# Routing of an audio tower's second expert mixture, worked off group by group within the attention before it

## The chip, the cores and the metric
One core of one Trainium2 chip. The metric is the device time of one execution in microseconds, the median of several runs. TensorE multiplies matrices (its granted clock is either 1.2 or 2.4 GHz; the profile gives it as a share of 2.4), VectorE and ScalarE work elementwise and reduce, GpSimd (POOL in the profile) works elementwise, more slowly, and issues indirect transfers, and the queue of SyncE (SP) issues the other transfers. Each engine has one queue and works it off in order; they wait for each other by semaphores.

## The reference, cut to what matters
64 sequences of 95 positions (96 in the kernel, one of padding) with 128 channels pass four layers. The kernel's first two phases do a token mixer, a retention layer and a first mixture; the change hardly touches them. Then come
```
h = h + attention(layernorm(h))   # over the 64 sequences at each position, 8 heads of 64
xf = layernorm(h).reshape(-1, 128)
z = swiglu5(xf @ shared_w1 + shared_b1) @ shared_w2 + shared_b2
w, idx = top_k(softmax(xf @ gate_w + gate_b), 2);  w = w / sum(w)
y = sum over the two chosen of 16 experts of w * (swiglu5(xf @ expert_w1 + b1) @ expert_w2 + b2)
h = h + y + z
```
Attention itself works across the batch: for one position the 64 sequences are queries and keys of each other. A position's result is final as soon as its step is done, so nothing in the mixture's norm and choice of experts has to wait for the other positions.

## The kernel before, in words
`hT` holds h in SBUF, channels on partitions, 64 x 96 tokens. `build` calls four phases one after the other; each is a block with a queue for every engine, and all engines meet at its end. At the start of a phase GpSimd clears the semaphores of the phase before.

**Attention** (`phase_attention`, L1432 to L1938) takes 4 positions, 256 tokens, a step: 24 steps. Body g of each engine's queue works at four steps at once: the scores and probabilities of step g, the projections of g + 1, the norm of g + 2 (`ln1`), and the output, the norm behind it (`ln2`) and the store of h of g - 1 and g - 2. `steps` writes out bodies 0 and 1, a hardware loop of ten pairs, and bodies 22 to 25. The order within a body is written by hand. What the prediction follows: TensorE's projections (L1549), scores (L1565 to L1576), turning and applying the probabilities (L1588, L1600), output product (L1611), and the turn of the normalised rows (`to_columns`, L660), which stands in the middle of the next scores; ScalarE's squares of the keys (L1683), normalisation (L1703) and its copy of h into `hg` (L1697); VectorE's keys (L1833, L1834), distances (L1841), shift (L1848 to L1852), probabilities (L1858 to L1864), store (L1884), scaled mean (L1890); GpSimd has only the inverse roots of two norms (L646).

**The second mixture** (`phase_second_mixture`, L1941 to L2630) first takes 12 groups of 512 tokens (8 positions of all 64 sequences) through this chain: ScalarE copies the group out of hT (`copy_in`, L2269), TensorE turns it into rows (L2155), VectorE takes mean and variance (`statistics`, L2420), GpSimd the inverse root (L2382), ScalarE normalises and repeats the rows (L2276, L2280), TensorE turns them into columns (L2164), ScalarE copies (`copy_x`, L2295), TensorE multiplies by the gate (`route`, L2173), VectorE finds the best two (`best`, L2439 to L2450, `chosen`, L2456 to L2468), TensorE counts the tokens before each one by a product with a triangle of ones (`prefix`, L2200), VectorE gets the positions of its 1024 rows in `slots` (`places`, L2478 to L2494), ScalarE the two shares by a sigmoid (L2287), and GpSimd sends the rows there with 8 indirect transfers (`send`, L2393). Each group's ranks build on the counts of the one before (`carry`). Beside this the shared expert is worked off: `shared_up` (L2182), `shared_clip` (L2500, L2502), `shared_silu` (L2301), `shared_act` (L2510), `shared_down` (L2192, and L2193, which adds h), `keep` (L2306). VectorE also prepares the experts' parameters, scales the weights (L2564), and SP writes them to DRAM (L2097). Behind the last group VectorE computes from the counts which expert each block of 128 rows belongs to (L2568 to L2591); TensorE turns this table, VectorE copies it out (L2595), and SP reads it.

Then come 111 blocks: SP loads rows and an expert's weights, TensorE turns the rows (`turn`, L2209), goes up (`ups`, L2217) and down (`down`, L2225), VectorE clips (L2607, L2608) and multiplies (L2616), ScalarE copies, does the SiLU (L2319) and scales (L2357), GpSimd sends the result back (L2400). The end adds the two rows of each token to the shared expert's result and stores it (L2627, L2629, L2081). The waits on `s_sent` hold the first load of rows until every row has been sent:
```
for sent in s_sent:
    sp.wait_ge(sent, 16 * 2 * GB * (NG // RX))
```

## Time and profile before
| | us |
|---|---|
| median of three runs | 2220.99 (2220.93 to 2224.79) |
| the profiled execution | 2223.54 |
| its span in the trace | 2221.7 |
| attention, from 1349.2 | 456.4 |
| second mixture up to its first block, from 1805.6 | 187.9 |
| 111 blocks, from 1993.5 | 192.1 |
| sums and stores at the end, from 2185.6 | 36.1 |

Over the span TensorE is busy for 87%, VectorE for 69%, ScalarE for 59%, GpSimd for 40%. The rest, up to 1349 us, is the two phases before. A row of a group of instructions gives line, engine, operation, what is written and read, shapes and count, then busy time and the mean of one, then the engine's idle time right before them and what ended it. A row in order of time begins with the start and the length in us; the bracket at its end is the idle time before it and its releaser. "PE" is TensorE's multiplication, "ACT" ScalarE, "DVE" VectorE. A wait that ends with "issue" or "remote" has no engine behind it that the profile shows.

### The profile page before, as it was taken

What the parts mean: (1) busy time and instruction counts of PE and PEld (TensorE: products, weight loads), DVE (VectorE), ACT (ScalarE), POOL (GpSimd) and SP (SyncE); (2) the same over time, 40 slices, a digit from 0 to 9 for tenths busy, and PEclk for the clock granted to TensorE, in tenths of its full rate; (3) what the DMA queues carried; (4) which work ended last, traced back from release to release, by engine and by line L of the source; (5) the groups of instructions that cost most, each with busy time, mean ns of one, the idle gap of its engine ahead of it and who ended that gap; (6) DMA issues with size and microseconds to landing.
All of it is one profiled execution on the core that took longest, in us unless ns stands there. A gap on an engine that the chain in (4) does not pass through costs nothing. (4 is left out here: it accounts for less than half of the span.)

```text
span 2221.7 us, 47490 instructions
## 1 busy us (share of the span) xinstructions
PE 1939.6 (87%) x16570; PEld 1359.7 (61%) x16570; DVE 1534.3 (69%) x3495; ACT 1312.7 (59%) x2355; POOL 891.5 (40%) x744
## 2 busy tenths in 40 slices
PE   5899999979998999999999997999999956657772
PEld 4678887845554566666666664666666634546661
DVE  4534455348886999999999984777777746645554
ACT  2445456445553677677767775777777746535551
POOL 0000000015553888888888882000000017655552
PEclk9999999989998999999999999999999967678876
DMA  8860010069920000000000000000000022126664
GB/s 281 321 234 29 21 30 11 1 239 411 413 94 11 10 11 10 10 10 10 10 10 10 10 10 22 2 0 0 0 0 0 1 50 90 43 67 183 183 181 176
DMA packets 87338, 177.84 MB, mean 80 GB/s; under 512 B 25917, under 2 KB 63214, under 8 KB 77846
## 3 DMA queue, kind: packets, MB, share of 16 engines
q1 hardware_dynamic: 78646, 160.11, 21.2%
q0 software_dynamic: 6624, 12.70, 1.7%
q10 hardware_dynamic: 1920, 3.11, 0.4%
q8 instruction: 86, 1.41, 0.3%
q14 instruction: 62, 0.51, 0.1%
HBM read 82.00 MB, written 94.86 MB: 80 GB/s over the span
## 5 line engine op out<-in xcount | busy, mean ns | idle before, releaser
L1146 ACT ACTIVATE b_pool_b<-b_pool_a,c_b 128x1024 f32<-128x1024 f32 x384 | 436.8, 1150 | 176.6 <-DVE b_pool_a L1379 153.9
L1216 POOL TENSOR_TENSOR b_pool_c<-b_pool_b 128x512 f32<-128x512 f32 x384 | 492.3, 1290 | 110.3 <-ACT b_pool_b L1146 64.8
L1379 DVE TENSOR_TENSOR b_pool_a<-b_p_s,c_shares 128x1024 f32<-128x1024 f32 x384 | 454.6, 1216 | 49.9 <-PE b_p_s L985 47.5
L983 PE MATMUL b_p_s<-c_x_hi,c_w_hi 128*128 128x512 f32 x384 | 296.4, 772 | 1.8 <-DVE b_pool_a L1379 1.8
L646 POOL TENSOR_TENSOR d_ln_rstd<-d_ln_var,d_ln_power 128x2 f32<-128x2 f32 x48 | 34.1, 711 | 418.9 <-DVE d_ln_var L642 414.0
L990 PE MATMUL b_p_y<-b_pool_c,c_w 128*128 128x512 f32 x384 | 196.7, 593 | 0.0
L990 PE MATMUL b_p_p<-b_pool_c,c_w 128*128 128x512 f32 x384 | 194.8, 591 | 0.0
L984 PE MATMUL b_p_s<-c_x_lo,c_w_hi 128*128 128x512 f32 x384 | 153.4, 399 | 0.0
L1268 DVE TENSOR_TENSOR b_pool_b<-b_p_s,b_decay 96x384 f32<-96x384 f32 x256 | 124.6, 546 | 41.5 <-PE b_p_s L854 41.3
L248 POOL COPY a_work<-a_vec 128x64 f32<-128x64 f32 x4 | 1.2, 306 | 378.5 <-PE a_p_A L339 222.9
L985 PE MATMUL b_p_s<-c_x_hi,c_w_lo 128*128 128x512 f32 x384 | 152.0, 396 | 0.0
L2400 POOL DMA_INDIRECT e_again<-e_by,e_xb x111 | 108.4, 977 | 92.0 <-ACT e_by L2357 50.9
L983 PEld LDWEIGHTS b_p_s<-c_x_hi,c_w_hi 128*128 128x128 f32 x384 | 73.3, 191 | 86.1 <-issue 77.2
L984 PEld LDWEIGHTS b_p_s<-c_x_lo,c_w_hi 128*128 128x128 f32 x384 | 73.6, 192 | 83.2 <-issue 83.0
L2393 POOL DMA_INDIRECT slots<-e_rows_x,e_pos x96 | 95.9, 999 | 39.9 <-issue 27.3
L1833 DVE TENSOR_SCALAR d_kk<-d_p_p,d_mu 128x256 f32<-128x256 f32 x96 | 46.0, 479 | 87.5 <-PE d_p_p L1549 87.5
L2319 ACT ACTIVATE e_bswish<-e_bgate,e_wb 96x128 f32<-96x128 f32 x111 | 54.8, 493 | 74.3 <-issue 49.2
L323 PE MATMUL a_p_A<-a_R,a_V 128*128 128x128 f32 x496 | 96.1, 275 | 0.0
L325 PE MATMUL a_p_A<-a_R,a_V 128*128 128x128 f32 x496 | 95.9, 275 | 0.0
L1176 POOL TENSOR_TENSOR b_yrs<-b_yve,b_power 96x32 f32<-96x32 f32 x15 | 81.4, 5427 | 35.0 <-DVE b_yve L1277 35.0
L527 DVE COPY a_work<-a_p_A 128x512 f32<-128x512 f32 (+1 forms) x32 | 21.6, 676 | 99.6 <-PE a_p_A L325 99.6
L985 PEld LDWEIGHTS b_p_s<-c_x_hi,c_w_lo 128*128 128x128 f32 x384 | 72.7, 189 | 18.8
(324 smaller groups left out, 4706.8 us busy)
## 6 DMA issues: line engine op xcount, KB each, us to landing
slots<-b_pool_c SPq DMA_DIRECT2D x55, 1040.0 KB
e_wb<-e_weights SPq DMA_DIRECT2D x111, 164.0 KB
band_scratch<-a_work SPq DMA_DIRECT2D x16, 1024.0 KB, 5.3
a_work<-band_scratch SPq DMA_DIRECT2D x16, 1023.5 KB, 7.6
a_raw<-in_Wc SPq DMA_DIRECT2D x16, 512.0 KB, 3.6
e_xb<-slots SPq DMA_DIRECT2D x111, 65.0 KB
c_shares<-c_share_lists SPq DMA_DIRECT2D x12, 512.0 KB, 3.8
e_yb<-e_again SPq DMA_DIRECT2D x12, 512.0 KB, 5.9
```

The source lines that it names most:

```text
L323: nc.tensor.matmul(bank[:, cols], V[:, j, :], R[:, f, 0:2 * NB], start=True, stop=False, skip_group_check=True)
L325: last = nc.tensor.matmul(bank[:, cols], V[:, j + 1, :], R[:, f, NB:3 * NB], start=False, stop=True, skip_group_check=True)
L983: nc.tensor.matmul(p_h[q % SLOTS][:, 0:WIDE], w1_hi[:, q, :], x_hi[s][:, :], start=True, stop=False)
L984: nc.tensor.matmul(p_h[q % SLOTS][:, 0:WIDE], w1_hi[:, q, :], x_lo[s][:, :], start=False, stop=False)
L985: nc.tensor.matmul(p_h[q % SLOTS][:, 0:WIDE], w1_lo[:, q, :], x_hi[s][:, :], start=False, stop=True)\
L990: nc.tensor.matmul(p_o[s][:, 0:WIDE], fw2[:, q, :], both[q % SLOTS][:, :], start=(q == 0), stop=(q == FQ - 1)).then_inc(s_down, 1)
L1146: nc.scalar.activation(hid[q % SLOTS][:, :, :], gelu_in[q % SLOTS][:, :, :], ACT.Gelu, bias=b1[:, q:q + 1]).then_inc(s_ge, 1)
L1216: nc.gpsimd.tensor_tensor(both[q % SLOTS][:, :], hid[q % SLOTS][:, 0, :], hid[q % SLOTS][:, 1, :], ALU.add).then_inc(s_bo, 1)
L1268: v.tensor_tensor(sm[n % 2][:, j, :], p_s[j][0:SP, 0:4 * SP], decay[:, j, :, :].rearrange("t a s -> t (a s)"), ALU.mult).then_inc(s_sm, 1)
L1379: v.tensor_tensor(gelu_in[q % SLOTS][:, :, :], p_h[q % SLOTS][:, 0:WIDE].unsqueeze(1).to_broadcast([128, 2, WIDE]), shares[s][:, :, :], AL ...
L2393: nc.gpsimd.indirect_dma_start(out=slots, out_offset=bass.IndirectOffsetOnAxis(ap=pos[g % RX][:, i * GB + n:i * GB + n + 1], axis=0), in_= ...
L2400: nc.gpsimd.indirect_dma_start(out=again, out_offset=bass.IndirectOffsetOnAxis(ap=xb[k % RL][:, 129:130].bitcast(U32), axis=0), in_=by[k % ...
```

## The change
The chain of the routing is moved into a class `Routing` with buffers of its own, which live through attention and the second mixture; xT and the rows (`acc`) are kept for all 12 groups. Attention's bodies are written out for all 26 values of g, and from g = 3 on they take up one step of the chain each: ScalarE copies group p out in body 2p + 3, TensorE turns it into rows in body 2p + 4 and into columns in 2p + 5, multiplies by the gate in 2p + 6 and counts in 2p + 7, and GpSimd sends in 2p + 8. GpSimd does what ScalarE and VectorE did of it: it normalises, repeats the rows, sums the choices, and adds the ranks; the shares come from a power of e (`exp_gap`) and a reciprocal instead of the sigmoid. Attention so takes groups 0 to 10 up to their columns, 0 to 9 up to their ranks and 0 to 8 up to their sends. The second mixture begins with the rest, and with the shared expert of groups 0 to 6 (`EARLY`); groups 7 to 11 of the shared expert are spread over the blocks, one in 18 blocks (`PACE`), with a PSUM bank of their own. The shared expert's h now comes from the rows in `acc`. Attention's first loads are 13 in place of 8, the second mixture's 5 in place of 10. The retention's semaphores are cleared within the last pass of the first mixture, and one more block of clears stands at the end. The diff, cut:
```diff
+                    if not after and q == 0:
+                        for signal in own:
+                            pool.sem_clear(signal)
...
+class Routing:
...
+    def copy_in(self, act, p):
+        if p >= 2:
+            act.wait_ge(self.s_t1, p - 1)
+        self.nc.scalar.copy(self.as_tokens(self.hg[p % 2][:, :]), self.tokens(p)).then_inc(self.s_hg, 1)
...
+    def keep_rows(self, act, p, bank):
+        act.wait_ge(self.s_t1, p + 1)
+        self.nc.scalar.copy(self.acc[:, p, :, :], bank[:, :].rearrange("p (n c) -> p n c", n=GB)).then_inc(self.s_kept, 1)
...
+    def inverse_root(self, pool, p):
+        pool.wait_ge(self.s_var, p + 1)
+        self.nc.gpsimd.tensor_tensor(self.rstd[:, :], self.var[:, :], self.power[:, :], ALU.pow).then_inc(self.s_rstd, 1)
...
+    def normalise(self, eng, e, p):
+        eng.wait_ge(self.s_rstd, p + 1)
+        eng.wait_ge(self.s_mv, p + 1)
+        self.free(eng, p)
+        for n in range(GB):
+            last = e.tensor_scalar(self.rows_x[p % self.RX][:, 0, n, 0:128], self.acc[:, p, n, :], self.mv[:, n, 0:1],
+                                   self.rstd[:, n:n + 1], ALU.subtract, ALU.mult)
+        last.then_inc(self.s_xn, 1)
...
+    def repeat_rows(self, eng, copy, p):
+        x = self.rows_x[p % self.RX]
+        eng.wait_ge(self.s_xn, p + 1)
+        copy(x[:, 1, :, 0:128], x[:, 0, :, 0:128]).then_inc(self.s_dup, 1)
...
+    def copy_x(self, act, p, bank):
+        act.wait_ge(self.s_t2, p + 1)
+        self.nc.scalar.copy(self.xT[p][:, :], bank[:, :]).then_inc(self.s_xT, 1)
...
+    def hots_before(self, eng, e, p):
+        eng.wait_ge(self.s_hots, p + 1)
+        for n in range(1, GB):
+            eng.wait_ge(self.s_upto, 4 * p + n)
+            e.tensor_tensor(self.upto[:, n + 1, :], self.upto[:, n, :], self.hots[:, n, :], ALU.add)\
+                .then_inc(self.s_upto, 1)
...
+    def exp_gap(self, pool, p):
+        pool.wait_ge(self.s_gap, p + 1)
+        if p >= 1:
+            pool.wait_ge(self.s_share, p)
+        self.nc.gpsimd.tensor_tensor(self.odds[:, :], self.euler[:, :], self.gap[:, :], ALU.pow).then_inc(self.s_odds, 1)
...
+    def ranks(self, eng, e, p):
+        eng.wait_ge(self.s_carry, 2 * p + 2)
+        eng.wait_ge(self.s_upto, 4 * p + 4)
+        e.tensor_tensor(self.rank[:, :, :], self.upto[:, 0:GB, :], self.base[:, :].unsqueeze(1).to_broadcast([self.ROWS, GB, E1]),
+                        ALU.add).then_inc(self.s_rank, 1)
...
+        e.tensor_tensor(self.mine[:, :, :, :].rearrange("p i n e -> p i (n e)"), self.hot[:, :, :, :].rearrange("p i n e -> p i (n e)"),
+                        self.rank[:, :, :].rearrange("p n e -> p (n e)").unsqueeze(1).to_broadcast([self.ROWS, 2, GB * E1]),
+                        ALU.mult).then_inc(self.s_mine, 1)
...
+    def places(self, dve, p):
+        v = self.nc.vector
+        dve.wait_ge(self.s_mine, p + 1)
+        v.tensor_reduce(self.posf[:, :], self.mine[:, :, :, :].rearrange("p i n e -> p (i n) e"), AX.X, ALU.add)\
+            .then_inc(self.s_posf, 1)
+        dve.wait_ge(self.s_posf, p + 1)
...
+        v.tensor_copy(self.pos[p % self.RX][:, :], self.posf[:, :]).then_inc(self.s_pos, 1)
...
+    def shares(self, dve, p):
+        v, x = self.nc.vector, self.rows_x[p % self.RX]
+        dve.wait_ge(self.s_odds, p + 1)
+        v.tensor_scalar(self.total[:, :], self.odds[:, :], 1.0, None, ALU.add).then_inc(self.s_total, 1)
+        dve.wait_ge(self.s_total, p + 1)
+        self.free(dve, p)
+        v.reciprocal(x[:, 0, :, 128], self.total[:, :]).then_inc(self.s_first, 1)
+        dve.wait_ge(self.s_first, p + 1)
+        v.tensor_tensor(x[:, 1, :, 128], x[:, 0, :, 128], self.odds[:, :], ALU.mult).then_inc(self.s_share, 1)
...
+    def send(self, pool, p, which=range(2 * GB)):
+        if 0 in which:
...
+        for at in which:
+            self.nc.gpsimd.indirect_dma_start(
+                out=self.slots, out_offset=bass.IndirectOffsetOnAxis(ap=self.pos[p % self.RX][:, at:at + 1], axis=0),
+                in_=self.rows_x[p % self.RX][:, at // GB, at % GB, :], in_offset=None, bounds_check=NSLOT - 1, oob_is_err=False)\
+                .then_inc(self.s_sent[p % self.RX], 16)
...
+def phase_attention(nc, sems, used, w, hT, ident, r):
...
         def steps(eng, body):
-            body(0, 0)
-            body(1, 1)
-            with eng.Fori(1, NSTEP // 2 - 1) as pair:
-                body(2 * pair, 0)
-                body(2 * pair + 1, 1)
-            for g in range(NSTEP - 2, NSTEP + 2):
+            for g in range(NSTEP + 2):
                 body(g, g % 2)
...
+            def routing(g):
+                p = g // 2 - 2
+                pe.wait_ge(s_vec, min(NT * g, NT * NSTEP))
+                if g % 2 == 0:
+                    if 0 <= p < r.NG:
+                        r.rows(pe, p, p_v)
+                    if p >= 1:
+                        r.route(pe, p - 1, p_pt)
+                else:
+                    if 0 <= p < r.NG:
+                        r.columns(pe, p, p_v)
+                    if p >= 1:
+                        r.prefix(pe, p - 1, p_pt)
...
+                        pair(2)
+                        if g >= 4:
+                            routing(g)
+                    scores(g, s, 1, between)
                 else:
-                    pair(2)
+                    routing(g)
                 pair(3)
...
                 if here:
+                    if g >= 6 and g % 2 == 0:
+                        pe.wait_ge(r.s_logit, g // 2 - 2)
+                    if g >= 6 and g % 2 == 1:
+                        pe.wait_ge(r.s_carry, 1 + 2 * (g // 2 - 2))
                     turn(g, 0)
                 if ahead:
                     values(g + 1)
                 if here:
+                    if g >= 4:
+                        pe.wait_ge(r.s_kept if g % 2 == 0 else r.s_xT, g // 2 - 1)
                     apply(g, s, 0)
...
+                if g >= 4 and g % 2 == 0:
+                    r.keep_rows(act, g // 2 - 2, p_v)
+                if g >= 4 and g % 2 == 1:
+                    r.copy_x(act, g // 2 - 2, p_v)
...
+                if g >= 3 and g % 2 == 1 and g // 2 - 1 < r.NG - 1:
+                    act.wait_ge(s_h, g - 1)
+                    r.copy_in(act, g // 2 - 1)
...
+            def routing(g):
+                p = g // 2 - 2
+                if g % 2 == 0:
+                    if p >= 2:
+                        r.send(pool, p - 2)
+                else:
+                    if 0 <= p < r.NG:
+                        r.inverse_root(pool, p)
+                        r.normalise(pool, nc.gpsimd, p)
+                    if p >= 1:
+                        r.hots_before(pool, nc.gpsimd, p - 1)
+                        r.exp_gap(pool, p - 1)
+                    if 0 <= p < r.NG:
+                        r.repeat_rows(pool, nc.gpsimd.tensor_copy, p)
+                        r.number_rows(pool, nc.gpsimd, p)
+                    if p >= 1:
+                        r.ranks(pool, nc.gpsimd, p - 1)
+            pool.wait_ge(r.s_set, r.SET)
+            pool.wait_ge(r.s_const, r.CONST)
             def body(g, s):
+                if g >= 4:
+                    routing(g)
...
+            def routing(g):
+                p = g // 2 - 2
+                if g % 2 == 0:
+                    if p >= 2:
+                        r.places(dve, p - 2)
+                        r.shares(dve, p - 2)
+                else:
+                    if 0 <= p < r.NG:
+                        r.statistics(dve, p)
+                    if p >= 1:
+                        r.choose(dve, p - 1)
+                        r.masks(dve, p - 1)
             def body(g, s):
...
                     store_h(g - 2)
+                if g >= 6 and g % 2 == 0:
+                    r.read_logits(dve, g // 2 - 3, p_pt)
+                if g >= 6 and g % 2 == 1:
+                    r.read_prefix(dve, g // 2 - 3, p_pt)
...
+        EARLY, PACE = 7, 18
...
+            def turn_table():
+                pe.wait_ge(s_more, 4)
+                pe.wait_ge(r.s_logit, NG)
+                nc.tensor.transpose(p_l[0:2, 0:MAXB], place[:, :], ident[0:MAXB, 0:MAXB]).then_inc(s_more, 1)
+            def late_up(g, j):
+                if j == 0:
+                    pe.wait_ge(s_sclipu, g)
+                else:
+                    pe.wait_ge(s_sclip, g + 1)
+                nc.tensor.matmul(p_s[0:FI, 0:N], sw1[:, j * FI:(j + 1) * FI], xT[g][:, :], start=True, stop=True)\
+                    .then_inc(s_sup, 1)
...
-            to_rows(0)
-            to_columns(0)
-            to_rows(1)
+            r.rows(pe, NG - 1, p_t)
+            r.route(pe, NG - 2, p_l)
...
+            shared_up(0)
+            r.columns(pe, NG - 1, p_x)
+            pe.wait_ge(r.s_logit, NG - 1)
+            r.route(pe, NG - 1, p_l)
+            r.prefix(pe, NG - 2, p_r)
+            shared_up(1)
+            pe.wait_ge(s_prep, 1)
+            shared_down(0)
+            pe.wait_ge(r.s_carry, 2 * (NG - 1) + 1)
+            r.prefix(pe, NG - 1, p_r)
+            for g in range(1, EARLY):
+                if g + 1 < EARLY:
+                    shared_up(g + 1)
+                if g == EARLY - 3:
+                    turn_table()
+                shared_down(g)
+            pe.wait_ge(s_tab, TABLE)
+            pe.wait_ge(r.s_carry, 2 * NG + 1)
+            pe.wait_ge(s_sclipu, EARLY)
             for k in range(MAXB + 3):
                 if k < MAXB:
                     turn(k)
...
                     ups(k - 1)
                 if k >= 3:
                     down(k - 3)
+                g = EARLY + k // PACE
+                if g < NG:
+                    if k % PACE == 4:
+                        late_up(g, 0)
+                    if k % PACE == 9:
+                        late_up(g, 1)
+                    if k % PACE == 15:
+                        shared_down(g)
...
+                g = EARLY + k // PACE
+                if g < NG:
+                    if k % PACE == 8:
+                        shared_silu(g)
+                    if k % PACE == 17:
+                        keep(g)
...
+            r.send(pool, NG - 3, range(0, 3))
+            r.inverse_root(pool, NG - 1)
+            r.exp_gap(pool, NG - 2)
+            r.send(pool, NG - 3, range(3, 2 * GB))
+            r.send(pool, NG - 2, range(0, GB))
+            r.exp_gap(pool, NG - 1)
+            r.send(pool, NG - 2, range(GB, 2 * GB))
+            r.send(pool, NG - 1)
             for k in range(MAXB):
                 send_back(k)
...
+            shared_clip(0)
+            r.read_prefix(dve, NG - 2, p_r)
+            r.ranks(dve, v, NG - 2)
+            r.places(dve, NG - 2)
+            r.shares(dve, NG - 2)
+            r.read_logits(dve, NG - 1, p_l)
+            r.choose(dve, NG - 1)
+            r.masks(dve, NG - 1)
+            r.hots_before(dve, v, NG - 1)
+            shared_act(0)
+            dve.wait_ge(s_w, 32)
+            v.tensor_tensor(blob[0:FI, :, DN:PR], blob[0:FI, :, DN:PR],
+                            prm[:, SCALE, 0:E1].unsqueeze(2).to_broadcast([FI, E1, 128]), ALU.mult).then_inc(s_prep, 1)
+            r.read_prefix(dve, NG - 1, p_r)
+            r.ranks(dve, v, NG - 1)
+            r.places(dve, NG - 1)
+            r.shares(dve, NG - 1)
+            shared_clip(1)
+            shared_act(1)
...
+            for g in range(2, EARLY):
+                shared_clip(g)
+                if g == EARLY - 2:
+                    dve.wait_ge(s_more, 5)
+                    v.tensor_copy(table[:, 0:MAXB], p_l[0:2, 0:MAXB]).then_inc(s_tab, 2)
+                shared_act(g)
...
+                g = EARLY + k // PACE
+                if g < NG:
+                    if k % PACE == 6:
+                        clip_gate(g, p_s)
+                    if k % PACE == 11:
+                        clip_lift(g, p_s)
+                    if k % PACE == 13:
+                        shared_act(g)
...
+            dve.wait_ge(s_acc, NG)
             for g in range(NG):
```

## Rows read from the trace of the kernel before
**Rows 1.** Busy time by stage: us, each engine (instructions), granted TensorE clock, DMA share, GB/s.
```profile
1349.20:1805.60 456.40, 430.49 (x6048) 298.64 (x6048) 324.53 (x888) 329.70 (x745) 34.28 (x50) 0.98 0.01 3
1805.60:1993.50 187.90, 110.78 (x481) 80.62 (x481) 108.36 (x651) 93.86 (x158) 108.88 (x114) 0.69 0.23 68
1993.50:2185.60 192.10, 137.44 (x777) 120.18 (x777) 107.57 (x333) 102.68 (x333) 108.41 (x111) 0.81 0.61 165
2185.60:2221.70 36.10, 0.00 (x0) 0.00 (x0) 16.35 (x24) 0.00 (x0) 0.00 (x0) 0.50 0.72 261
```

**Rows 2.** The tile with group positions: duration min/median/max in ns, first and last start.
```profile
L2494 DVE CAST e_pos<-e_posf x12: 171/172/292, 1833.8 to 1973.3; 128x8 uint32<-128x8 f32 x12
```

**Rows 3.** VectorE in order of time, one group's choice: start, us, instruction.
```profile
1903.86 0.41 DVE L2443 MAX8 e_top<-e_logit 128x8 f32<-128x16 f32 x4
...
1904.54 0.89 DVE L2420 BATCH_NORM_STATS2 e_stats<-e_p_t 128x6 f32<-128x128 f32 x4
...
1907.72 0.59 DVE L2468 TENSOR_TENSOR e_upto<-e_upto,e_hots 128x16 f32<-128x16 f32 x3
```

**Rows 4.** The page's costliest groups, GpSimd: busy us, mean ns, idle before.
```profile
L2393 POOL DMA_INDIRECT slots<-e_rows_x,e_pos x96 | 95.9, 999 | 39.9 <-issue 27.3
...
L1216 POOL TENSOR_TENSOR b_pool_c<-b_pool_b 128x512 f32<-128x512 f32 x384 | 492.3, 1290 | 110.3 <-ACT b_pool_b L1146 64.8
```

**Rows 5.** Order of time, from the last count to the first block.
```profile
1974.06 0.16 DVE L2568 TENSOR_TENSOR e_count<-e_carry,e_first 128x16 f32<-128x16 f32 x1
...
1980.21 0.16 DVE L2591 TENSOR_TENSOR e_place<-e_place,e_starts 111x1 f32<-111x1 f32 x1 [0.46 <-DVE e_place L2589]
...
1987.47 0.26 DVE L2595 CAST e_table<-e_p_l 2x111 uint32<-2x111 f32 x1 [4.33 <-remote]
...
1988.45 0.80 PE L2192 MATMUL e_p_a<-e_sw,e_sact 97*128 97x128 f32 x2 [6.47 <-DVE e_sact L2510]
...
1992.17 0.59 ACT L2306 COPY e_acc<-e_p_a 128x512 f32<-128x512 f32 x1 [4.22 <-PE e_p_a L2193]
...
1993.55 0.30 PE L2209 MATMUL e_p_t<-identity,e_xb 128*128 128x128 f32 x1 [1.41 <-DMA e_xb<-slots]
```

**Rows 6.** TensorE in order of time, one pass of the group loop.
```profile
1910.96 1.91 PE L2182 MATMUL e_p_g<-e_xT,e_sw 128*96 128x512 f32 x2
...
1913.90 0.96 PE L2173 MATMUL e_p_l<-e_wg,e_xT 128*128 128x16 f32 x8
1914.71 0.63 PE L2155 MATMUL e_p_t<-identity,e_hg 128*128 128x128 f32 x4
1915.18 0.39 PE L2192 MATMUL e_p_a<-e_sw,e_sact 97*128 97x128 f32 x2
```

**Rows 7.** The tile of attention's distances, as rows 2.
```profile
L1841 DVE SCALAR_TENSOR_TENSOR d_dist<-d_p_s,d_r x48: 681/691/693, 1373.1 to 1785.9; 128x512 f32<-128x512 f32 x48
```

**Rows 8.** Groups of instructions behind 1370 us: busy us, mean ns, idle before, releaser.
```profile
L1833 DVE TENSOR_SCALAR d_kk<-d_p_p,d_mu 128x256 f32<-128x256 f32 x92 | 44.1, 479 | 83.2 <-PE d_p_p L1549 83.2
...
L2269 ACT COPY e_hg<-hT 128x512 f32<-128x512 f32 x12 | 12.8, 1075 | 1.0 <-PEq L1435 1.0
```

**Rows 9.** Order of time, where two bodies of attention meet, and later.
```profile
1564.03 0.81 ACT L1703 ACTIVATE d_ln_xn<-d_p_t,d_nmr,d_ln_rstd 128x128 f32<-128x128 f32 x2
...
1564.13 0.17 DVE L642 TENSOR_SCALAR d_ln_var<-d_ln_mv 128x2 f32<-128x2 f32 x1
...
1564.89 0.44 PE L660 MATMUL d_p_t<-identity,d_ln_xn 128*128 128x128 f32 x2 [0.23 <-ACT d_ln_xn L1703]
...
1572.56 0.59 PE L1549 MATMUL d_p_p<-d_ln_xT,d_wk 128*128 128x256 f32 x2
```

**Rows 10.** Two tiles that VectorE writes in the first mixture, as rows 2.
```profile
L1307 DVE TENSOR_TENSOR c_x_lo<-c_ln_xT,c_x_hi x12: 693/1784/1789, 701.1 to 1267.4; 128x512 fp32r<-128x512 f32 x12
...
L618 DVE COPY c_ln_hg<-hT x12: 412/1393/1398, 678.3 to 1244.8; 128x512 f32 x10, 128x512 f32<-128x512 f32 x2
```

**Rows 11.** GpSimd in order of time, attention's last inverse root.
```profile
1801.73 0.70 POOL L646 TENSOR_TENSOR d_ln_rstd<-d_ln_var,d_ln_power 128x2 f32<-128x2 f32 x1 [9.30 <-DVE d_ln_var L642]
```

537 lines of the change are left out of this document (233 added, 304 removed).

## Prediction
> **What bounds the kernel now.** I read the stretches by stage first, then the groups of instructions, then the instructions in order of time where two stages meet. The stretches show four stages behind the first mixture [rows 1]. Attention takes 456.4 us and TensorE works 430.5 of them at a granted clock of 0.98 (practically its upper level, 2.4 GHz): TensorE bounds it. VectorE has 324.5 us of work, ScalarE 329.7, GpSimd 34.3. Then come 187.9 us before the first block of the second mixture, in which no engine works more than 111 us: a chain between engines, twelve groups long, with GpSimd's 96 sends beside it. The blocks take 192.1 us, the sums at the end 36.1. The change carries most of the second stage into the first, where GpSimd stands idle and the others have a fifth to a quarter of their time free. So it is a question of how much of what is carried over meets a cover there.
>
> **What is taken out: the 187.9 us.** In the new order groups 0 to 10 have been normalised and groups 0 to 8 sent when attention ends; groups 9, 10 and 11 are still sent, and 7 of the 12 groups of the shared expert worked off, before the first block. I build the new stretch from the old one's pieces, with t for its start.
> - To the positions of the last group: the old stage needs 28 us until group 0 has its positions (1833.8 less 1805.6) [rows 1, 2], and has the set-up, one norm and the work on the experts' parameters in it. The new one has the same norm (group 11), the same set-up, and two choices (10 and 11) in place of one, each 3.9 us of VectorE less the statistics [rows 3], but no second norm. I take t + 28.
> - Sends: (95.9 + 27.3)/96 = 1.28 us each [rows 4]. 24 of them are 31 us; the last 8 can start at t + 28 and end at t + 39, which nothing waits for.
> - One clip and activation of the shared expert, 2.5 us, then the table of blocks: 1974.06 to 1980.37, 6.3 us [rows 5]. t + 37.
> - Then the loop over shared groups 2 to 6, with TensorE in it as the bound: going up 2.94 us (1910.96 to 1913.90), going down with the kept rows 3.7 us at 1.2 GHz (1988.45 to 1992.17), 1.8 us at the upper level by half of that [rows 5, 6]. A mean of 5.5 us a group; four of them before TensorE is free for the first block: t + 59. The table is copied out before the last two, at t + 53, and from that to the first block are 6.1 us (1987.47 to 1993.55) [rows 5]: t + 59 too. I take 60.
> The gain is 187.9 - 60 = 128 us. Bounds: 45 us if TensorE stays at its upper level and no gap opens; 85 us if all seven groups run at 7 us and two gaps come like the 4.3 us before the copy of the table, for which the trace names no engine [rows 5].
>
> **What is put into attention.** A body lasts (1785.9 - 1373.1)/23.5 = 17.6 us [rows 7]. Two bodies carry one group, about ten such pairs. Per pair:
> - TensorE, the bound, so every instruction counts: four transposes to rows and four to columns, 0.47 us each four (1914.71 to 1915.18); the logits 0.81 us (1913.90 to 1914.71) [rows 6]; the two rank products are four instructions against the logits' eight, 0.4 us. 2.2 us. Its waits I count at nothing: the columns and ranks come behind the third pair of projections, which ends at 1573.1 in a body where VectorE is free from 1564.3 [rows 9], and statistics, root, normalisation and sums before them take some 6 us. Gone that cover of 3 us, each wait would stand in full.
> - ScalarE: the copies of rows and of columns stand before the squares of the keys, where it has slack of that size. The copy out of hT, 1.08 us [rows 8], stands in odd bodies between the vector copy and the second squares; behind these waits the normalisation, and for it TensorE, which already idles 0.23 us there [rows 9]. Nothing covers this: 1.1 us.
> - VectorE: in odd bodies statistics, choice and masks come ahead of the keys, from 1903.86 to 1907.72 without the three sums: 3.9 us [rows 3]. The cover is the wait for the first key product, 83.2 us over 23 bodies, 3.6 us each [rows 8]. 0.3 us stick out. In even bodies (positions, shares, under 1.5 us) nothing does.
> - GpSimd: eight sends in even bodies, 10.2 us, between two inverse roots 15 us apart; in odd bodies two powers of 1.0 us, the normalisation and repetition of 128x512 and some small sums. The nearest row for a pass over 128x512 is 1.29 us [rows 4]; about 7 us in all, behind which only the next inverse root queues. Its time is covered, not what it does to VectorE. Beside that same GpSimd pass VectorE's sum of two SBUF tiles takes 1.78 us against 0.69 alone, and its copy 1.39 against 0.41 [rows 10]. So one meeting costs up to 1.09 us. Bounds per pair: 0, if they miss each other; 4.4 for four of the large two-input passes (two shifts, two probabilities). GpSimd's passes come early in the body, where one shift and one probability lie, both started with queues behind them: I take one full wait, 1.1 us.
> The sum is 2.2 + 1.1 + 0.3 + 1.1 = 4.7 us a pair, 47 us. By the Trainium skill ("SBUF — State Buffer", Who interferes with whom) a VectorE instruction in a 2-port mode or with two SBUF inputs and a GpSimd instruction that reads SBUF exclude each other for the whole instruction; by that rule alone, with no slack in between, the term would be nearer 4.4 a pair and the sum 33 us higher. The trace agrees on the single wait, not yet on how many there are.
> - Attention's end: the rows and logits of body 24 stand before the output product and run at the low clock, 2 us. In body 25 3.9 us of VectorE stand before the last mean, of which the inverse root's 0.7 is hidden [rows 3, 11]: 3 us. The last rank sums follow the last store: 2 us. Together 7. GpSimd's eight sends of body 24 fit into the 9.3 us it idles there [rows 11].
> - The loop becomes straight code. The two unrolled ends of the old loop run at the pace of its middle, so I count nothing; a fetch that comes late would show as a gap with no engine behind it.
> - Semaphores cleared within the first mixture's last pass instead of at attention's start: no row shows a clear; taken as 0, bounds -3 and +3.
>
> **What is put into the blocks.** Five groups of the shared expert: TensorE 5 x 5.5 = 28 us, VectorE and ScalarE less. TensorE idles 192.1 - 137.4 = 54.7 us of the blocks [rows 1], but in gaps that a block's own chain makes. Bounds 0 and 28; between them I take 12, since GpSimd's 1.28 us a send is the pace of the bursts and takes up the smaller delays. One more clearing section at the end, 1 us.
>
> **Sum.** Against the profiled execution of 2223.5 us (span 2221.7): -128 + 47 + 7 + 12 + 1 = -61, 2162.5. The median of the runs shown is 2220.99, 2.5 us under that execution: 2160.
>
> **Rivals.**
> A. Attention covers more: only TensorE's own 2.2 us a pair count, since VectorE catches up while TensorE does the added work. 25 us less: 2135. For it: all other engines have over a quarter free. Against: the 0.23 us that TensorE already waits at the normalisation [rows 9].
> B. The stretch before the blocks stays long, 85 us: low clock (0.69 there now [rows 1]) and gaps. 2185.
> C. TensorE's 28 us come out in full in the blocks, its queue being in order: 2176.
> D. Slower than before: in odd bodies VectorE has some eleven passes or small sums with two SBUF inputs beside about ten GpSimd instructions. At 1.09 us a wait [rows 10], seven waits a pair instead of one eat up the 61 us; twelve give 120 us more, 2280. This is what the skill's rule would do if the two engines meet at nearly every instruction. Against it: GpSimd's streaming work is at most 5 us of 35 a pair, and small instructions hold little.
> E. The change does not do what it says, because a group's send waits on into the next stage: then GpSimd's sends of up to 31 us would still lie before the blocks, which is B.
>
> **Chances.** Forecast 0.45, A 0.17, B 0.17, C 0.12, D 0.09. A measurement of this kernel tells 0.2% from no change, 4.4 us; of D I give 0.07 to slower and 0.02 to no change. The range takes in A to C and two of them together: 2115 to 2215.
>
> **What would show it.** Attention 50 to 58 us longer, its TensorE busy 22 us more; in odd bodies VectorE's two-input passes with means above 0.69; ScalarE's copy ahead of a TensorE wait near 1.3 us in every second body; 72 sends inside attention with idle gaps of the inverse root still there; first block 60 us after attention; blocks 200 to 206 us. A wrong count of waits shows in VectorE's mean times; a wrong second term in a gap before the copy of the table or in the clock. If attention grew by more than 110 us, the whole forecast would be wrong.

## The result, and the profile after

The changed kernel takes 2208.06 us (median of ten runs, 2201.11 to 2215.58), the kernel before 2221.24 beside it (2216.6 to 2224.79). The ratio is 0.9938 [0.9926, 0.995]: faster by 0.6%, 13 us, where 61 were forecast. The direction is right, the time lies within the range, the gain is less than a quarter of the forecast one. The profiled execution took 2209.61 us, its span is 2207.7.

First the stages of the changed kernel, as [rows 1]: attention, the stretch up to the first block, the blocks, the end; then two bodies of attention, the second with eight sends in it.
```profile
1345.30:1914.50 569.20, 493.19 (x6256) 348.63 (x6256) 377.50 (x1333) 351.10 (x778) 191.35 (x267) 0.90 0.04 13
1914.50:1972.40 57.90, 42.44 (x174) 28.68 (x175) 39.86 (x157) 14.99 (x22) 28.75 (x27) 0.67 0.46 136
1972.40:2170.80 198.40, 145.59 (x879) 116.33 (x877) 116.66 (x348) 109.24 (x344) 109.98 (x111) 0.90 0.59 160
2170.80:2207.70 36.90, 0.00 (x0) 0.00 (x0) 16.43 (x24) 0.00 (x0) 0.00 (x0) 0.50 0.71 255
1674.97:1694.71 19.74, 19.29 (x272) 13.72 (x275) 17.33 (x75) 14.09 (x32) 8.48 (x13) 1.00 0.01 2
1694.71:1720.76 26.05, 21.86 (x262) 15.81 (x255) 14.72 (x46) 15.08 (x34) 10.43 (x12) 0.87 0.07 22
```
| us | before | after | difference | forecast |
|---|---|---|---|---|
| up to attention | 1349.2 | 1345.3 | -3.9 | 0 |
| attention | 456.4 | 569.2 | +112.8 | +54 |
| up to the first block | 187.9 | 57.9 | -130.0 | -128 |
| blocks | 192.1 | 198.4 | +6.3 | +12 |
| end | 36.1 | 36.9 | +0.8 | +1 |

Everything but attention came out close to its term. There the forecast has 22 us of new TensorE time; the stage's row has 62.7 more (493.19 less 430.49), and a clock of 0.90 where it had 0.98. Two bodies next to each other tell more than the stage: the first is full of TensorE's work (19.29 of 19.74 us, clock 1.00), the second has 4.2 us without any and a lower clock. The two differ by GpSimd's eight sends. The stores of h, one a body, show the rhythm (before, the first twenty distances are 17.85 to 17.87):
```profile
1647.57 0.67 DVE L2221 TENSOR_TENSOR hT<-d_y,hT 128x256 f32<-128x256 f32 x1
1674.97 0.64 DVE L2221 TENSOR_TENSOR hT<-d_y,hT 128x256 f32<-128x256 f32 x1
1694.71 0.67 DVE L2221 TENSOR_TENSOR hT<-d_y,hT 128x256 f32<-128x256 f32 x1
1720.76 0.65 DVE L2221 TENSOR_TENSOR hT<-d_y,hT 128x256 f32<-128x256 f32 x1
1740.30 0.66 DVE L2221 TENSOR_TENSOR hT<-d_y,hT 128x256 f32<-128x256 f32 x1
```
27.4, 19.7, 26.1, 19.5: here a body without sends is 1.7 to 1.9 longer than before, one with sends 8.2 to 9.5.

The groups of instructions that answer to [rows 8] and [rows 4] say what ended the waits, and that the large passes of two SBUF tiles kept their length:
```profile
L2170 DVE TENSOR_SCALAR d_kk<-d_p_p,d_mu 128x256 f32<-128x256 f32 x92 | 44.0, 479 | 110.6 <-remote 69.7 <-PE d_p_p L1826 40.9
L1704 POOL DMA_INDIRECT slots<-r_rows_x,r_pos x96 | 99.2, 1033 | 47.5 <-issue 28.1 <-DVE r_rows_x L1695 19.3
L2189 DVE SCALAR_TENSOR_TENSOR d_dist<-d_dist,d_d_low 128x512 f32<-128x512 f32 x48 | 33.3, 693 | 1.6
L2201 DVE TENSOR_TENSOR d_prob<-d_dist,d_p_inv 128x512 f32<-128x512 f32 x48 | 33.4, 695 | 1.9 <-DVE d_p_inv L2197 0.2
```
Before, all 83.2 us of VectorE's wait for the key product were ended by TensorE [rows 8]. Now 69.7 of 110.6 end with "remote": nothing on record is behind them. In order of time, a body with sends:
```profile
1797.43 1.12 POOL L1704 DMA_INDIRECT slots<-r_rows_x,r_pos  x1 [0.97 <-DVE r_rows_x L1695]
...
1798.44 0.40 PE L1853 MATMUL d_p_s<-d_q_rows,d_q_sq 64*64 64x128 f32 x8
...
1798.85 0.97 POOL L1704 DMA_INDIRECT slots<-r_rows_x,r_pos  x1 [0.30 <-issue]
...
1799.70 0.59 PE L1826 MATMUL d_p_p<-d_ln_xT,d_wk 128*128 128x256 f32 x2
1800.12 0.97 POOL L1704 DMA_INDIRECT slots<-r_rows_x,r_pos  x1 [0.30 <-issue]
1801.40 0.97 POOL L1704 DMA_INDIRECT slots<-r_rows_x,r_pos  x1 [0.31 <-issue]
1801.62 0.60 ACT L2027 ACTIVATE d_r<-d_p_s 128x512 f32<-128x512 f32 x1 [3.33 <-DMA a_work<-in_x_tok]
...
1802.49 0.48 DVE L2170 TENSOR_SCALAR d_kk<-d_p_p,d_mu 128x256 f32<-128x256 f32 x1 [5.93 <-remote]
```
The scores end at 1798.84; ScalarE, which waits for them, idle for 3.33 us, begins at 1801.62. (The DMA that its bracket names is a load of the kernel's first phase and can't be it.) The keys' product ends at 1800.29, VectorE takes it up at 1802.49. TensorE then waits for both. So work that TensorE has done reaches its readers 2 to 3 us late, several times while the eight sends run, and the clock falls in the gaps.

The trace also records when a semaphore is raised. The one behind the scores is raised 2.8 us after their end, the one behind the keys' product 2.1 us after, and both readers begin within 0.2 us of that. So the readers wake at once, and the delay lies between TensorE's product and its signal. In attention before (1370 to 1800), none of 488 such signals of TensorE comes more than 0.05 us late; in the changed kernel (1370 to 1900) 61 of 525 come 1 to 7 us late. Of the 1598 signals of the other three engines there, 1557 come within 0.02 us; the other 41 have no record within 7 us, which a missing record would give as well. One caution: the ends of TensorE's products are modelled by the profiler, so a late signal and a product that really ended late look alike.

At attention's end stands one more piece that no term had:
```profile
1907.86 0.45 POOL L1674 TENSOR_TENSOR r_mine<-r_hot,r_rank 128x128 f32<-128x128 f32 x1
1914.52 0.33 SPq L2400 DMA_DIRECT2D e_par<-in_epar  x1
1914.54 1.06 ACT L1527 COPY r_hg<-hT 128x512 f32<-128x512 f32 x1 [8.08 <-PEq L1716]
```
From 1908.3 to 1914.5 no engine works. The trace has one record there, the DRAIN with which GpSimd ends the block (the drain from here on): 6.46 us, against 0.80 before.

### The profile page after: what moved, and what is told of

Read it like the earlier page. It is cut to its first block and busy times, and to the rows that moved or that the text cites. A ratio compares the mean times of both kernels' runs of the same rounds, so it can differ in the third digit from the quotient of the medians.

```text
span 2207.7 us, 46828 instructions
## 1 busy us (share of the span) xinstructions
PE 1939.2 (88%) x16570; PEld 1352.1 (61%) x16570; DVE 1526.5 (69%) x3461; ACT 1261.6 (57%) x2263; POOL 969.4 (44%) x874
## 5 line engine op out<-in xcount | busy, mean ns | idle before, releaser
L2632 POOL DMA_INDIRECT e_again<-e_by,e_xb x111 | 110.0, 991 | 104.3 <-ACT e_by L2606 65.8
L2170 DVE TENSOR_SCALAR d_kk<-d_p_p,d_mu 128x256 f32<-128x256 f32 x96 | 46.0, 479 | 116.2 <-remote 69.7
L984 PEld LDWEIGHTS b_p_s<-c_x_lo,c_w_hi 128*128 128x128 f32 x384 | 73.7, 192 | 82.5 <-issue 82.3
L1704 POOL DMA_INDIRECT slots<-r_rows_x,r_pos x96 | 99.2, 1033 | 47.5 <-issue 28.1
L1848 PE MATMUL d_p_s<-d_kk,d_qq 64*64 64x128 f32 x1536 | 89.7, 287 | 0.3 <-issue 0.3
```

The lines of the kernel that those rows point to most:

```text
L984: nc.tensor.matmul(p_h[q % SLOTS][:, 0:WIDE], w1_hi[:, q, :], x_lo[s][:, :], start=False, stop=False)
L1704: self.nc.gpsimd.indirect_dma_start(out=self.slots, out_offset=bass.IndirectOffsetOnAxis(ap=self.pos[p % self.RX][:, at:at + 1], axis=0), ...
L2632: nc.gpsimd.indirect_dma_start(out=again, out_offset=bass.IndirectOffsetOnAxis(ap=xb[k % RL][:, 129:130].bitcast(U32), axis=0), in_=by[k % ...
```

## Experiments

Two theories at first. **Sends**: eight indirect transfers in a row hold back what TensorE reports. **Straight code**: the instructions of 26 written-out bodies are fetched late, which I had counted as nothing. Four kernels on one chip, the kernel before at 2218.45 beside them, cross the two. In e1, e3 to e6 and e16 GpSimd (in e4 SP) also writes zeros to a tensor that nothing reads; what the kernel computes is unchanged. Each of e1 to e6 and of e16 has one run. On the chip of e1 to e6 the kernel before took 2218.45 once beside e1 to e4 and 2222.34 to 2234.66 in the 19 runs beside e5 and e6, so their whole times compare only to some 10 us. Attention by itself is steadier (456.4 before, 457.9 in e2, 457.4 in e4), and the price of a send is taken from it.

**e1_loop_sends**: the old kernel with its loop, and eight transfers in every even body.
```diff
+                    for at in range(2 * GB):
+                        nc.gpsimd.indirect_dma_start(
+                            out=junk, out_offset=bass.IndirectOffsetOnAxis(ap=ids_j[:, at // GB, at % GB:at % GB + 1], axis=0),
+                            in_=rows_j[:, at, :], in_offset=None, bounds_check=2 * NB * SP - 1, oob_is_err=False)
```


> The kernel before, its hardware loop kept, with eight indirect transfers by GpSimd of 128 rows of 520 bytes each, to a DRAM tensor that nobody reads, at the head of the even bodies 0 to 20 of attention (11 groups of eight). Nothing waits for them but GpSimd's next group. Theory 1 (beside a group of such transfers the consumers of TensorE's results start late, some 7 us a group, as in the even bodies after the change): attention 456 + 11 x 7 = 533 us, the whole near 2298. Theory 2 (the straight code fetches instructions, and the fetch is what comes late beside the transfers): here no fetch is needed in the loop, so attention stays at 456 to 461, the whole near 2223. Theory 3 (the added work of VectorE and GpSimd is what holds the even bodies up): no change, near 2223.

2305.1 us, +86.7; attention 549.9.

**e2_straight**: the old kernel written out.
```diff
-            with eng.Fori(1, NSTEP // 2 - 1) as pair:
-                body(2 * pair, 0)
-                body(2 * pair + 1, 1)
-            for g in range(NSTEP - 2, NSTEP + 2):
+            for g in range(NSTEP + 2):
                 body(g, g % 2)
```


> The kernel before with attention's 26 bodies written out instead of the hardware loop, nothing else. All theories: 456 us of attention, 2221 us in all, within 4 us. If straight code alone is slower, by 10 us or more, that part of the growth of attention is the code's and not the routing's.

2220.37, +1.9; attention 457.9, 1.5 longer: the stores of h are 17.93 apart instead of 17.87. Straight code costs next to nothing.

**e3_straight_sends**: both edits.


> Attention's bodies written out and the same 11 groups of eight indirect transfers. Theory 1 (transfers alone): the same 533 us of attention as with the loop, 2298 in all. Theory 2 (late instruction fetch): 533 us here and 456 with the loop. Theory 3: 456.

2310.07, +91.6; attention 546.8.

**e4_straight_direct**: as e3, but SP sends the same 88 tiles by direct transfers.
```diff
+                    sp.dma_start(junk[row:row + 128, :], rows_j[:, at, :]).then_inc(s_junk, 16)
```


> Attention's bodies written out, and in place of GpSimd's indirect transfers the same 88 tiles go to the same DRAM tensor as direct transfers issued by SP, released in the same even bodies. Theory 1 in its narrow form (it is GpSimd's indirect transfer that delays): attention 456 us, 2221 in all. In its wide form (any transfer whose completions are counted, or any traffic of that size): 533 and 2298.

2221.9, +3.5; attention 457.4. Attention in e3, then in e4, and VectorE's wait for the key product in e1, e3 and e4:
```profile
1348.90:1895.70 546.80, 477.57 (x6048) 325.62 (x6048) 326.14 (x888) 330.72 (x746) 122.64 (x150) 0.90 0.05 15
```
```profile
1349.40:1806.80 457.40, 431.15 (x6048) 297.79 (x6048) 323.35 (x888) 329.22 (x745) 34.48 (x51) 0.98 0.06 17
```
```profile
L1852 DVE TENSOR_SCALAR d_kk<-d_p_p,d_mu 128x256 f32<-128x256 f32 x92 | 44.1, 480 | 165.3 <-remote 83.3 <-PE d_p_p L1555 82.1
```
```profile
L1847 DVE TENSOR_SCALAR d_kk<-d_p_p,d_mu 128x256 f32<-128x256 f32 x92 | 44.1, 480 | 163.7 <-remote 99.4 <-PE d_p_p L1550 64.3
```
```profile
L1844 DVE TENSOR_SCALAR d_kk<-d_p_p,d_mu 128x256 f32<-128x256 f32 x92 | 43.9, 478 | 86.2 <-PE d_p_p L1557 86.2
```
GpSimd's drain is 7.85 us in e1 and e3, 7.05 over the old one, but not all of it shows. Before, the other engines work on for 3 us behind GpSimd's last instruction, and the next phase begins 0.3 us behind the last store of h; in e1 and e3 it begins 4.5 us behind it. So the drain costs 4.2 us. The rest of what attention grew by is (549.9 - 456.4 - 4.2)/88 = 1.01 us a send in the loop and (546.8 - 457.9 - 4.2)/88 = 0.96 in straight code. The bytes are innocent: e4 moves the same tiles at 17 GB/s and has no "remote". Nothing on the path waits for these transfers, so it isn't their data either.

**e5_loop_four**: e1 with four transfers in a row in place of eight.


> As the first kernel (loop kept, 11 groups in the even bodies), but four transfers a group in place of eight. There 88 transfers cost 86.7 us, 1.0 us each. Theory 1a (each transfer costs TensorE's consumers about the same): 44 x 1.0 = 44 us more than before, 2262. Theory 1b (the first of a group are harmless, the delay comes with a long burst): clearly less than 30 us, under 2248. Theory 1c (a fixed price for every group): near 80 us, 2300.

2269.69 against 2228.75, +41. Attention 500.6; the drain is 4.26, and 0.6 of it shows: (500.6 - 456.4 - 0.6)/44 = 0.99 a send. A short burst costs as much per send as a long one.

**e6_straight_paced**: e3, where each of the eight waits for one more projection.
```diff
+                        pool.wait_ge(s_proj, 10 * (g + 1) + at + 1)
```


> As the third kernel (straight code, 11 groups of eight), but each transfer of a group waits for one more of the body's eight projections, so the eight are spread over the body instead of standing in one burst. Theory 1a (a price per transfer): still near 90 us more than before, 2310. Theory 1b (a burst is what hurts): under 30 us more, below 2250.

2262.76, +34; attention 492.7, so (492.7 - 457.9 - 4.2)/88 = 0.35 a send. GpSimd and ScalarE in order of time:
```profile
1607.27 0.96 POOL L1820 DMA_INDIRECT d_junk<-d_rows_j,d_ids_j  x1 [1.37 <-PE d_p_p L1550]
...
1608.54 0.97 POOL L1820 DMA_INDIRECT d_junk<-d_rows_j,d_ids_j  x1 [0.30 <-issue]
...
1610.14 0.96 POOL L1820 DMA_INDIRECT d_junk<-d_rows_j,d_ids_j  x1 [0.63 <-issue]
1611.41 0.97 POOL L1820 DMA_INDIRECT d_junk<-d_rows_j,d_ids_j  x1 [0.30 <-issue]
1613.27 0.60 ACT L1723 ACTIVATE d_r<-d_p_s 128x512 f32<-128x512 f32 x1 [3.05 <-remote]
```
The projections end in pairs, so the transfers still came in pairs 1.27 us apart, and behind two such pairs ScalarE waited. The same number a body for a third of the price: what matters is the spacing, and not its mean, which is 1.67 us here.

**e7_eight_later**: the changed kernel, with the sends of group 8 moved behind attention.
```diff
-                    if p >= 2:
+                    if 2 <= p < r.NG - 2:
                         r.send(pool, p - 2)
```


> The changed kernel with the eight transfers of group 8 moved from body 24 of attention to the head of the second mixture, where GpSimd sits idle for 11.6 us. Body 24 is at attention's end, where the engines wait for each other anyway, so the gain is less than the 7 us that a group costs in the middle: 3 to 8 us off the changed kernel's 2208, near 2202. If the transfers cost nothing there: 2208. If the last transfers, ending later, hold up the first block: 2208 to 2215.

2223.86, ratio 0.9977 [0.9963, 0.9992]: less gain than the change itself. Attention is 1 us shorter in this execution, but the stretch before the blocks went from 57.9 to 66.1. GpSimd, with t = 1917.1:
```profile
1930.59 0.97 POOL L1704 DMA_INDIRECT slots<-r_rows_x,r_pos  x1 [0.30 <-issue]
1931.57 1.07 POOL L1557 TENSOR_TENSOR r_rstd<-r_var,r_power 128x4 f32<-128x4 f32 x1
```
The inverse root of group 11 now stands behind eight sends, at t + 14.5; in the changed kernel it runs at 1923.60, t + 9.1. GpSimd's queue is in order, and the last group's chain goes through it. The 3 to 8 us that were expected off the changed kernel did not come.

**e8_seven_eight_later**: groups 7 and 8, with six buffers of rows.


> As the kernel before it, with group 7's eight transfers moved there too (six row buffers in place of four): another 7 us off attention, body 22 being in its full course; against it 40 transfers of 1.28 us, 51 us, now fill the 58 us before the first block, whose first load waits for the last of them. Theory 1 with room before the blocks: near 2196. If the transfers become the bound there: 2200 to 2206.

2228.52, ratio 1.0002 [0.9989, 1.0015], no gain over the kernel before at all; attention 560.5, but 78.0 before the blocks. Moving bursts out of attention doesn't help; they must be broken up where they are.

**e9_paced_even**: the changed kernel, with the sends of groups 0 to 7 laid between the projections of the even body, 1.3 to 3.7 us apart.
```diff
+                        for at, done in ((1, 2), (2, 4), (3, 6), (4, 8)):
+                            pool.wait_ge(s_proj, 10 * (g + 1) + done)
+                            r.send(pool, p - 2, [at])
```


> The changed kernel with group 0's to group 7's transfers spread over their even body: one at its head, four behind the second, fourth, sixth and eighth projection, two more before the first inverse root and one between the two roots. Spread transfers cost 0.39 us each beside the old loop's work, a burst 1.0. By that 64 transfers give back 64 x 0.5 = 32 us: 2208 - 32 = 2176, a ratio to before of 0.980. Theory 1a (a fixed price per transfer): no gain, 0.994. Rival: the inverse roots, now queued behind transfers, come late and the body grows by that: 0.994 or more.

2151.71, ratio 0.9698 [0.9682, 0.9715]: 32 us off the changed kernel were expected, some 53 came. One distance in seven is 1.27 us even so; a single short one costs nothing that shows.

**e10_paced_pair**: the same over both bodies of a pair, 3.2 us and more apart but for one short distance in group 7.


> The same, but over two bodies: four in the even body behind its head and projections 4, 6 and 8, one between its roots, and three in the odd body, around the ranks and between the roots. If it is the density that counts, nearly the whole price goes: some 50 us off the changed kernel's 2208, 2158, a ratio of 0.972. If a transfer has a price of its own (0.4 us) whatever its distance: as the kernel before it, 0.980.

2146.72, ratio 0.9662 [0.9642, 0.9682]. Attention of e10, and the wait for the key product:
```profile
1353.60:1860.60 507.00, 456.48 (x6256) 324.83 (x6256) 374.96 (x1333) 350.55 (x779) 198.71 (x267) 0.96 0.05 14
```
```profile
L2181 DVE TENSOR_SCALAR d_kk<-d_p_p,d_mu 128x256 f32<-128x256 f32 x92 | 43.9, 477 | 57.3 <-PE d_p_p L1826 57.3
```
The same instructions on every engine, 62 us less, TensorE's busy time 37 us less, its clock 0.96, and no "remote" left; one of TensorE's 525 signals is more than 1 us late. So more than half of the price is that TensorE runs slower. 62.2 us over 64 sends are 0.97 each, what e1, e3 and e5 give. With bursts attention varies, though: the same code takes 562.3 in e12, which makes it 55 us, 0.86 each.

**e11_copy_behind**: the changed kernel, ScalarE's copy out of hT behind the normalisation instead of ahead of it.
```diff
-                if g >= 3 and g % 2 == 1 and g // 2 - 1 < r.NG - 1:
-                    act.wait_ge(s_h, g - 1)
-                    r.copy_in(act, g // 2 - 1)
                 if ahead:
...
+                if g >= 3 and g % 2 == 1 and g // 2 - 1 < r.NG - 1:
+                    act.wait_ge(s_h, g - 1)
+                    r.copy_in(act, g // 2 - 1)
```


> The changed kernel with ScalarE's copy of a group out of hT (1.1 us) moved from before the squares to behind the normalisation of the odd body. In the trace TensorE waits 1.2 us for the normalised rows in every even body and 0.2 us in every odd one; if that copy is the cause, ten pairs give back 1.0 us each: 2198, a ratio of 0.989. If the copy only moves on to delay ScalarE's copy of the columns at the next body's head: 0.994 as it was.

2209.53, ratio 0.9945 [0.9927, 0.9963]: no gain. Ahead of the first sends the distances between stores fall from 18.9 to 17.9 and from 19.4 to 18.4, the 1.0 us that was expected; further on the pairs take no less than before, with 26.0 to 26.5 us in a body with sends and 20.1 to 22.5 in one without, which mostly had 19.5.

**e12_all_early**: all twelve shared groups ahead of the blocks.
```diff
-        EARLY, PACE = 7, 18
+        EARLY, PACE = 12, 18
```


> The changed kernel with EARLY at 12: the shared expert's last five groups are worked off before the blocks again. The blocks, 198 us with them and 192 in the old kernel, should be back at 192 (6 us less); the stretch before the first block, 58 us, grows by 5 groups at 3.5 to 5.5 us, 18 to 28. Sum: 12 to 22 us more than the changed kernel, 2220 to 2230, a ratio of 0.999 to 1.004. If the late groups have cost more in the blocks than 6 us (by hiding a gain that the clock gave), the blocks fall below 190.

2217.18, ratio 0.9976 [0.9966, 0.9987]. 15.8 us longer before the blocks (73.7), 5.0 shorter in them (193.4):
```profile
1985.50:2178.90 193.40, 127.64 (x779) 107.30 (x777) 107.74 (x333) 102.84 (x334) 108.18 (x111) 0.90 0.60 164
```
Five shared groups cost 16 us ahead of the blocks and less in them. How much less the profiles don't settle, since the blocks with the same code take 198.4 in the changed kernel, 193.5 in e11 and 196.2 in e10; by the medians (0.9976 against 0.9938) the split pays about 8 us.

**e13_paced_and_copy**: e10 and e11 together.


> The kernel that spreads the transfers over two bodies (ratio to before 0.966), with ScalarE's copy out of hT behind the normalisation too. Alone in the changed kernel that move took 1.0 us from each body without transfers and nothing from the whole, since the bodies with a burst took it up. Without bursts it should come out in full: ten bodies at 1.0 us, 10 us, ratio 0.962. If it is taken up by something else: 0.966.

2146.83, ratio 0.9633 [0.9613, 0.9652], on a chip where the kernel before takes 2227.61. Attention is 500.0, 7 less than in e10, but the blocks, whose code is the same, took 206.2 in this profile. The ratio is 0.3% lower than e10's with intervals that meet: the 10 us expected can't be seen. A pair of bodies takes 38.6 to 38.9 us in place of 39.1 to 39.4, so that the 1.0 us a pair comes back only in part.

The blocks' own send-backs (L2632) come at 1.28 us too, in bursts. **e14_blocks_pause** lets GpSimd fill 256 columns behind each, **e15_blocks_longer_pause** 512.
```diff
                 send_back(k)
+                if k > 0:
+                    pool.wait_ge(s_pause, k)
+                nc.gpsimd.memset(pause[:, 0:256], 0.0).then_inc(s_pause, 1)
```


> As the kernel before it, with a fill of a private tile (about 0.3 us) behind each of the 111 transfers that send a block's rows back, so that two of them are at least 1.45 us apart instead of 1.28. The blocks last 196 us now, 1.77 a block, in bursts of about four transfers and a stall of nearly 2 us. If density beside TensorE makes those stalls, they shrink or go and the blocks last 165 to 185 us; if 1.45 us is still too dense, 196; if the stalls have another cause (the blocks' own chain), the pause only adds: 196 to 205.

> The same with a fill twice as long: transfers at least 1.65 us apart, 111 x 1.65 = 183 us for the blocks if the stalls are gone; 196 and more if they have another cause.

2141.54 (ratio 0.9621 [0.9601, 0.9641]) and 2139.67 (0.9606 [0.959, 0.9622]). The send-backs of e15, then its blocks:
```profile
2001.28 0.97 POOL L2644 DMA_INDIRECT e_again<-e_by,e_xb  x1 [0.17 <-issue]
2002.24 0.54 POOL L2661 MEMSET e_pause<- 128x512 f32 x1
2002.95 0.97 POOL L2644 DMA_INDIRECT e_again<-e_by,e_xb  x1 [0.17 <-issue]
```
```profile
1907.20:2100.20 193.00, 129.34 (x879) 104.04 (x877) 116.72 (x348) 111.56 (x344) 169.20 (x222) 0.94 0.61 164
```
The blocks are 192.1 in e14 and 193.0 in e15, there with GpSimd longer at work than before (169.20 us of 193.00) and TensorE's clock higher. The 165 to 185 us of the first branch did not come: the density of the sends isn't what stalls the blocks. There was little of it to take: in the changed kernel's blocks 4.7 us of waits end with "remote", in e10's 1.9. And 193.5 to 206.2 us for one code (e11, e10, e13) say that a profile can't show 3 us here. The medians fall by 5.3 and 7.2 us against e13. The intervals overlap, though all four runs of e15 (2138.56 to 2140.64) are below all four of e13 (2143.09 to 2149.46): a small gain over e13 is likely and not more, and what it comes from isn't shown. e15 is the fastest version, 3.9% below the kernel before where the change as made gives 0.6%.

**e16_straight_gap** asks for the price of spacing alone: e3 with a fill of 512 columns behind every transfer.


> The old kernel, straight code, with the 11 groups of eight transfers that cost 90 us in a burst at 1.28 us, now with a fill of half a microsecond behind each, 1.65 us apart, and no other wait. If the distance alone decides, most of the 90 us go: under 25 us more than before, under 2245. If being released by TensorE's progress is what helped, and not the distance: still 60 to 90 us more, 2280 to 2310.

2235.0 against 2227.61, +7.4; attention 464.4. The transfers, then VectorE's wait:
```profile
1621.37 1.03 POOL L1819 DMA_INDIRECT d_junk<-d_rows_j,d_ids_j  x1 [0.16 <-issue]
1622.41 0.54 POOL L1825 MEMSET d_pause_j<- 128x512 f32 x1
1623.13 0.97 POOL L1819 DMA_INDIRECT d_junk<-d_rows_j,d_ids_j  x1 [0.17 <-issue]
```
```profile
L1850 DVE TENSOR_SCALAR d_kk<-d_p_p,d_mu 128x256 f32<-128x256 f32 x92 | 44.1, 479 | 78.5 <-PE d_p_p L1550 78.5
```
Without the fill 91.6 us more than the kernel before, with it 7.4; no "remote" is left. All that the fill does is to make the distance 1.7 us instead of 1.28. Of the 6.5 us by which attention is longer than e2's, 4.2 are the drain (7.85 us here too), which leaves 0.03 a send. In e6 the mean distance is the same, with every second one at 1.27, and a send costs 0.35: it is short distances in a row that cost, not the mean.

## Why the prediction was right and wrong, step by step

- **The stretch before the blocks, 60 us: right (57.9).** Its pieces too: the last group's positions at t + 28 (1942.2, t + 27.7), the table copied out at t + 53 (1964.93, t + 50.4). The clock stayed low there (0.67), as rival B had it, but at 42.44 us of TensorE's work in 57.9 it cost no more than was counted. B is out, and with it E.
- **The pairs in attention, 4.7 us each: 3.4.** In e10, without bursts, the distances between stores from body 3 to body 23 grew by 34 us together. TensorE's instructions, 2.2: e10 has 26.0 us more than the kernel before (456.48 less 430.49), over ten and a half pairs 2.5. The copy of h, 1.1: e11 got 1.0 ahead of the first sends by moving it. VectorE's choice, 0.3: no run isolates it.
- **The port wait, 1.1 a pair: it came, but on the other engine.** All 48 shifts took 691 to 694 ns and of 48 probabilities the longest took 832, so VectorE paid next to nothing. But in each of the eight odd bodies of groups 0 to 7, GpSimd's power (`exp_gap`) begins 0.02 us behind the shift and takes 1.56 to 1.57 us, where alone it takes 1.00 to 1.06:
```profile
1690.97 0.69 DVE L2189 SCALAR_TENSOR_TENSOR d_dist<-d_dist,d_d_low 128x512 f32<-128x512 f32 x1
1690.99 1.57 POOL L1647 TENSOR_TENSOR r_odds<-r_euler,r_gap 128x4 f32<-128x4 f32 x1
...
1924.66 1.00 POOL L1647 TENSOR_TENSOR r_odds<-r_euler,r_gap 128x4 f32<-128x4 f32 x1
```
The long normalisation misses the two (1687.06 to 1690.25 in the first of the two bodies above; shift and probability begin at 1690.97 and 1693.32). So the trace agrees with the rule of the Trainium skill ("SBUF — State Buffer", Who interferes with whom) that the two exclude each other; the prediction erred in who waits. GpSimd came second and had time to spare, so it cost nothing, and the 33 us more that the rule would give by itself didn't come. D is out as a mechanism, though something of D's size did happen.
- **Attention's end, 7 us: 10, and the drain.** In e10 the last two distances grew by 7.4 us, and the ranks end 2.4 us behind the last store. The drain adds 5.9. So attention's 50.6 us of growth in e10 are 44.7 without the drain, against 47 + 7 forecast: the pairs 13 us too dear, most of it the port wait, the end 3 too cheap.
- **The blocks, 12 us: 6.3.** C (28 us in full) is out. At the same clock of 0.90, the changed kernel has 18.0 us more of TensorE's work in the blocks than e12 (145.59 less 127.64) and takes 5.0 longer, so TensorE's gaps took up most of the five groups, within the spread of these stages. I had named GpSimd's pace as the cover; e15 says otherwise, since with longer pauses on GpSimd the blocks got no longer. Against the kernel before, TensorE's busy time rose by only 8.2 us, since its clock was 0.81 there. Why it is higher now, with and without the five groups, isn't shown.
- **Straight code, nothing: right**, 1.5 us of attention in e2. **Clears, 0: right.** The -3.9 of the table is spread: attention begins between 1346.7 and 1349.4 in the eight profiles with the old clears, and between 1345.3 and 1353.6 in the ten with the new ones.
- **The step that failed** is GpSimd's, in "What is put into attention": "eight sends in even bodies, 10.2 us, between two inverse roots 15 us apart ... Its time is covered, not what it does to VectorE." What it does to the readers of TensorE I never priced. Measured: 569.2 - 507.0 = 62 us for 64 sends, more than the 48 us by which the gain fell short. The block's drain, 6 us, wasn't listed at all. 62 + 6 - 9 is the 59 us between +112.8 and +54.
- **How it could have been read.** The kernel before sends at the same 1.28 us ahead of its blocks [rows 4], and the wait that I set aside as a gap "for which the trace names no engine" is this one: VectorE's copy of the table, 4.33 us, "remote", started at 1987.47 [rows 5]. It reads what TensorE turned at 1981.63, while the last sends ran:
```profile
1981.62 0.97 POOL L2393 DMA_INDIRECT slots<-e_rows_x,e_pos  x1 [0.30 <-issue]
...
1981.63 0.34 PE L2250 MATMUL e_p_l<-identity,e_place 111*2 111x111 f32 x1 [5.09 <-DVE e_place L2591]
1982.90 0.97 POOL L2393 DMA_INDIRECT slots<-e_rows_x,e_pos  x1 [0.30 <-issue]
1984.17 0.97 POOL L2393 DMA_INDIRECT slots<-e_rows_x,e_pos  x1 [0.30 <-issue]
```
TensorE was done at 1981.97, its signal was raised at 1987.38, 5.4 us later, with TensorE idle before and after: dense work of TensorE's isn't needed for it. In the changed kernel the sends are over by then (the last starts before 1956), and the same copy follows its product without a wait:
```profile
1964.00 0.26 PE L2484 MATMUL e_p_l<-identity,e_place 111*2 111x111 f32 x1
...
1964.93 0.25 DVE L2764 CAST e_table<-e_p_l 2x111 uint32<-2x111 f32 x1
```
All profiles agree: in the eight with the old second mixture (before, e1 to e6, e16) this signal is raised 3.8 to 8.0 us behind its product, in the ten others 0.02 at most.
- **The last sentence of the prediction** had attention growing by more than 110 us as the sign that the whole forecast would be wrong. It grew by 112.8, and the forecast wasn't wrong as a whole: one mechanism was missing, and e9 and e10, which take it away, give -70 and -75 us against -61 forecast.

**Still open.** Which resource delays TensorE's signals isn't shown, nor why those of the other engines aren't seen late. The runs exclude the bytes moved (e4), the transfers' data, written-out code (e2) and the need for more than four in a row (e5). GpSimd's own waits for a projection end with "remote" too, in e6. Not tried: even distances between 1.28 and 1.67 us inside attention (1.46 only in the blocks, e14), other densities of TensorE's instructions, smaller transfers.
